# Three of thirteen row one-hot columns made by GpSimd in the routing stage of a graph layer kernel

## The reference, cut to what matters

```python
hi, hj = h[ei], h[ej]                      # ei = src, ej = dst, 103125 edges
m = silu(concat(hi, hj, d2) @ mW1 + mb1)
m = silu(layer_norm(m, ln_g, ln_b) @ mW2 + mb2)
agg = segment_sum(m, ei, 3125)             # sum of the messages of each source node
y = h + silu(concat(h, agg) @ uW1 + ub1) @ uW2 + ub2
...                                        # x + y, then top-k nodes, gelu feed-forward, sum
```

## Time and profile before

| | |
|---|---|
| Runs of the kernel before | 2300.64, 7235.58 and 2305.55 us; median 2305.55 |
| The profiled execution, its time | 2300.03 us |
| The profiled execution, its span | 2298.3 us |
| Busy time, share of the span | PE 2029.3 (88%), DVE 1999.2 (87%), ACT 1385.4 (60%), POOL 1035.3 (45%) |
| Mean granted TensorE clock | 0.947 of full speed |
| First and last scatter of the routing | issued at 192.90 and 411.24 us |

### The profile page before, as it was taken

How to read it: one execution, slowest core, us unless ns; L and a number is a source line. 1 busy time by engine, 2 the same in 40 slices (tenths; PEclk the granted TensorE clock), 3 DMA queues, 4 the chain that set the end, 5 groups by cost and what they waited for, 6 DMA issues and landing times. The chain is left out here.

```text
span 2298.3 us, 51635 instructions
## 1 busy us (share of the span) xinstructions
PE 2029.3 (88%) x11892; PEld 1711.3 (74%) x11893; DVE 1999.2 (87%) x6778; ACT 1385.4 (60%) x2909; POOL 1035.3 (45%) x1037
## 2 busy tenths in 40 slices
PE   3555764499999999999999999999999998799996
PEld 2324553388888888888888888888888886677775
DVE  6899999599999999999999999999999999736795
ACT  1112331388888888787777777777777776423331
POOL 8752222555555555555555555555555556203000
PEclk9987776599999999999999999999999999899998
DMA  3000000432222222222222222222222222010001
GB/s 122 0 1 24 25 25 17 147 94 71 73 71 73 69 73 72 70 73 71 71 73 69 72 71 71 73 71 71 73 71 71 71 70 59 1 40 1 28 1 56
DMA packets 65908, 135.17 MB, mean 59 GB/s; under 512 B 20973, under 2 KB 36451, under 8 KB 65606
## 3 DMA queue, kind: packets, MB, share of 16 engines
q0 software_dynamic: 42016, 111.40, 17.0%
q1 hardware_dynamic: 22577, 22.31, 3.1%
q10 hardware_dynamic: 1266, 0.83, 0.2%
HBM read 124.33 MB, written 10.16 MB: 59 GB/s over the span
## 5 line engine op out<-in xcount | busy, mean ns | idle before, releaser
L862 POOL DMA_INDIRECT g_rows<-b_table,idx_pair x834 | 790.4, 948 | 733.0 <-DVE idx_pair L1014 591.6
L984 PE MATMUL ps<-w2g,nT 128*128 128x256 f32 x3336 | 789.1, 379 | 0.0
L984 PEld LDWEIGHTS ps<-w2g,nT 128*128 128x128 f32 x3336 | 601.5, 190 | 64.5
L899 ACT ACTIVATE normed<-act,shift,rstd_e 128x255 f32<-128x255 f32 x834 | 453.8, 596 | 196.7 <-DVE shift L1086 196.2
L1023 DVE TENSOR_TENSOR agg<-psG,agg 125x256 f32 x834 | 348.4, 418 | 121.6 <-PE psG L967 41.5
L967 PE MATMUL psG<-msg,ohf 128*125 128x256 f32 x1668 | 430.1, 380 | 0.0
L1129 DVE BATCH_NORM_STATS2 stat_e<-act 128x6 f32<-128x256 f32 x834 | 313.8, 423 | 0.0
L958 PE MATMUL psH<-a_sb,ohT 128*128 x1668 | 304.4, 305 | 0.0
L920 ACT ACTIVATE nT<-psM 128x512 f32<-128x512 f32 x417 | 249.0, 597 | 90.1 <-PE psM L976 88.9
L967 PEld LDWEIGHTS psG<-msg,ohf 128*125 128x125 f32 x1668 | 283.9, 187 | 25.1 <-ACT msg L916 0.2
L1122 DVE TENSOR_TENSOR g_rows<-psH,g_rows 128x512 f32<-128x512 f32 x417 | 289.4, 694 | 11.5 <-DMA g_rows<-b_table,idx_pair 8.5
(11 more groups left out here) (201 smaller groups left out, 2406.1 us busy)
## 6 DMA issues: line engine op xcount, KB each, us to landing
g_rows<-b_table,idx_pair POOLq DMA_INDIRECT x834
h_sb<-in_x SPq DMA_DIRECT2D x1, 3125.0 KB
b_table<-b_out SPq DMA_DIRECT2D x25, 125.0 KB
x_all<-in_x SPq DMA_DIRECT2D x1, 3125.0 KB
out<-x_all SPq DMA_DIRECT2D x5, 625.0 KB
rec_d<-rec SPq DMA_DIRECT2D x1, 1668.0 KB, 8.7
agg<-rec_d SPq DMA_DIRECT2D x6, 256.0 KB, 4.2
row<-score_d SPq DMA_DIRECT2D x1, 1525.9 KB
```

The lines of the kernel that those rows point to most:

```text
L862: pool.indirect_dma_start(g_rows[:, j, n, :], None, b_table[:, :], bass.IndirectOffsetOnAxis(ap=idx_pair[:, j, n:n + 1], axis=0)).then_inc ...
L899: ins = nc.scalar.activation(normed[:, (j - 9) % 2, n, 0:D - 1], act1[:, (j - 9) % RING, n, 0:D - 1], ACT.Identity, scale=rstd_e[:, 1 - fa ...
L984: mm = pe.matmul(ps2[:, k, n, :], nT[:, k, n, q, :], w2g[:, q, :], start=(q == 0), stop=(q == 1))
```

## The change: what it does

Of the thirteen row one-hot columns of a group VectorE now makes the first ten, still in one instruction. The last three are made by GpSimd with one `tensor_scalar` per column, which compares the constant row of 0 to 127 (`iota_n`) with the edge's row number, one number per partition. They go to a ring of four, `orp`, that lies in the memory of `f1` and `f2`, which are free by then. `route(s)` waits for both makers. GpSimd makes the columns of groups 0 to 3 as soon as `r_all` and `q_all` are complete (`s_places`), ahead of its `jump` steps, and the columns of group s+4 right behind the issue of scatter s; from group 4 on it first waits for the matmuls of the group that used the ring's place.

```diff
+PCOLS = 3
+PRING = 4
...
-            or_ = sb("or_", [P, 2, COLS, P], BF16)
+            or_ = sb("or_", [P, 2, COLS - PCOLS, P], BF16)
+            orp = [half[:, k * PCOLS * P // 2:(k + 1) * PCOLS * P // 2].bitcast(BF16).rearrange("p (t r) -> p t r", t=PCOLS)
+                   for half in (f1, f2) for k in range(PRING // 2)]
...
+                def pool_columns(s):
+                    if s >= PRING:
+                        pool.wait_ge(s_win, s - PRING + 1)
+                    for k in range(PCOLS):
+                        c = s * COLS + COLS - PCOLS + k
+                        ins = pool.tensor_scalar(orp[s % PRING][:, k, :], iota_n[:, :], r_all[:, c:c + 1], None,
+                                                 ALU.is_equal)
+                    ins.then_inc(s_orp, 1)
+
+                pool.wait_ge(s_places, 1)
+                for s in range(PRING):
+                    pool_columns(s)
                 pool.wait_ge(s_upto, 1)
...
                     pool.indirect_dma_start(rec_d[:, :], bass.IndirectOffsetOnAxis(ap=dest[:, s:s + 1], axis=0),
                                             recw[:, s % 4, :, :].rearrange("p w n -> p (w n)"), None).then_inc(s_scat, 16)
+                    if s + PRING < SUPERS:
+                        pool_columns(s + PRING)
...
                 def route(s):
                     pe.wait_ge(s_or, s + 1)
+                    pe.wait_ge(s_orp, s + 1)
...
-                        mm = pe.matmul(psK[:, s % 3, 0:PLANES * WIN], or_[:, s % 2, t, :],
+                        marks = or_[:, s % 2, t, :] if t < COLS - PCOLS else orp[s % PRING][:, t - COLS + PCOLS, :]
+                        mm = pe.matmul(psK[:, s % 3, 0:PLANES * WIN], marks,
...
-                link(V.tensor_tensor(q_all[:, :], place[:, :], f2[:, :], ALU.subtract))
+                V.tensor_tensor(q_all[:, :], place[:, :], f2[:, :], ALU.subtract).then_inc(s_places, 1)
+                dve.wait_ge(s_places, 1)
...
-                    V.tensor_tensor(or_[:, s % 2, :, :], r_all[:, own].unsqueeze(2).broadcast_to([P, COLS, P]),
-                                    iota_v.unsqueeze(1).broadcast_to([P, COLS, P]), ALU.is_equal)
+                    mine = slice(s * COLS, (s + 1) * COLS - PCOLS)
+                    V.tensor_tensor(or_[:, s % 2, :, :],
+                                    r_all[:, mine].unsqueeze(2).broadcast_to([P, COLS - PCOLS, P]),
+                                    iota_v.unsqueeze(1).broadcast_to([P, COLS - PCOLS, P]), ALU.is_equal)
```

More of the change, by code:

```diff
@@ L223, in build @@
             s_or = sem("s_or")
+            s_orp = sem("s_orp")
+            s_places = sem("s_places")
             s_win = sem("s_win")
```

## The result

The changed kernel takes 2291.68 us (median of 5 runs, 2288.62 to 2293.51), the kernel before 2303.69 in the same series (median of 5 runs, one of which took 7235.58): a ratio of 0.995, 95% interval 0.9934 to 0.9965. So it is faster beyond the noise, but by far less than two per cent, and the forecast of "same" (0.96) came. The forecast time was 2292, range 2281 to 2303. The profiled execution took 2292.16 us, its span is 2290.4.

The account below looks back on a forecast made before the run. VectorE and TensorE's chain of tables at its lower clock were taken to set alternate pairs. Pairs -9.9, columns at the end +1.4, groups 50 to 52 -1.2, start +1.8 gave -7.9 us: 2292, range 2281 to 2303.

Parts of the forecast that it names:

- VectorE's comparison: Row one-hots at L714: 384 of 1664 elements go, 0.397 us less a group, at most 24.6 us over 62 groups.
- The pairs: Middle of the routing, 21 pairs: 11 set by VectorE gain 0.79 us each, 10 by TensorE 1.2 together; 9.9 gained.
- the bound that I gave (12.8): Middle of the routing: 12.8 us gained over the 21 pairs if all TensorE-set pairs last 7.40 us.
- Rival 1: The 21 pairs: TensorE's clock stays up, all last 6.70 us, 20.2 us gained instead of 9.9, time 2282; chance 13%.
- The start: Up to `low(3)`: GpSimd's columns and a lock make it 1.8 us later; bounds 0.2 earlier to 5 later.
- The lock on w2g: Start, L749: two VectorE operations beside GpSimd's 2.8 to 3.0 us steps lose 0 to 5.6 us; 2 taken.
- The columns at the end: Last scatters: five issues with columns behind them, 2.75 us apart against 2.47, lose 1.4 us.
- The end: Groups 50 to 52 gain 1.2 us; VectorE's gain in 53 to 61 is lost to ScalarE's 12.21 us and nine scatters.
- 4: Routing groups: VectorE stands behind GpSimd's columns, kernel over 2% slower, 83 us, time 2383; chance 3%.
- 3: Routing: GpSimd sets the pace from 0.8 us a column on; at 1.0 us the time is 2320; chance 6%.
- 2: The 21 pairs: the clock stays down, every pair lasts 8.22 us, 11.7 us slower, time 2314; chance 4%.
- 5: Whole routing: nothing is left, slow pairs lengthen and the start costs its full 5 us, 2299 to 2303; chance 12%.

Follow-up runs that it names:

- e: The kernel before, with 30 extra matmuls filling TensorE's idle stretch in even groups and all from 50 on: ratio 0.9989 to the kernel before.
- f: The changed kernel with 30 extra matmuls filling TensorE's idle stretch: ratio 0.9942 to the kernel before, 13.6 us less.
- c: The changed kernel without GpSimd's columns, a constant zero matrix in their place (edges of three columns left out): ratio 0.9916 to the kernel before.
- d: The changed kernel with VectorE making all thirteen columns again and GpSimd its three as well: ratio 1.0037 to the kernel before, 7.7 us more.
- a: The changed kernel with VectorE's two w2g operations moved from behind group 2 to behind group 5: ratio 0.9937 to the kernel before.
- h: The changed kernel with the w2g operations behind group 5 and a ring of eight: ratio 0.9925 to the kernel before, 18.6 us less.
- i: The changed kernel again, unaltered, on another chip beside the kernel before: ratio 0.9958, 10.5 us less.
- k: The changed kernel with ScalarE's three small DMAs issued by SyncE instead: ratio 0.9946 to the kernel before, 11.5 us less.
- b: The changed kernel with a ring of eight, columns of groups 4 to 7 made ahead of the first scatter: ratio 0.9929 to the kernel before.
- g: The changed kernel with two columns on GpSimd and eleven on VectorE: ratio 0.9958 to the kernel before, 9.6 us less.
- l: The changed kernel with w2g later, ring of eight, 30 extra matmuls in even groups below 50, small DMAs on SyncE: ratio 0.9918 to the kernel before.

## Why the prediction was right, step by step

*VectorE's comparison*: right, 0.398 us a group against 0.397.

*The pairs*: right in mechanism, mis-sized: 17.3 us against 9.9, and the bound that I gave (12.8) was passed. VectorE's pairs went to 6.70 as said, and eleven of them at 0.79 make the 8.7 us of the sum. The ten that TensorE sets were to give the 1.2 us that they had in hand, and gave 8.6: the mistake was to hold the slow pairs' length fixed. The sign that I gave for it, 1.4 us of waiting in front of `low`, did not come; it is 0.19. A slow pair is as long as the clock stays low in it, and that is no constant of the work: e and f show that the clock costs 3.1 us before and 2.6 after over all 21 pairs, so that VectorE's own 16.8 us (157.82 - 141.02) came through whole, with 0.5 more. c shows that the columns have no part in it, d that the old pattern returns with VectorE's old length. The traces of a, h, i and k have orders of slow pairs different from each other and from after, b and c the order of after, and their sums are all 143.5 to 143.9 us, though i is the same program; with eleven columns on VectorE (g) the clock costs more, 150.86 against some 146.7 of VectorE's own (21 x 6.955 + 0.65). Why the sums agree so well at ten columns is open. Rival 1, the clock stays up, did not come true as a whole: where every second idle stretch is 2.43 us, the clock is low behind it. But for eight pairs of a, and some of k, it did, with stretches of 2.15 us and a clock of 1.00; a pair of 8.13 us then ended it. The gain is nearer to this rival's 20.2 than to 9.9.

*The start*: right in place, too small: 4.9 us against 1.8, just within the bound of 5. The lock on w2g took 4.0 us, within my bounds of 0 and 5.6, of which I took 2; a gives 3.9 back. Its length alone is no price: in i the two operations took 3.44 us and ended at 180.91, as after (180.93), since they end with GpSimd's step. The twelve columns took 10.10 us where I had 7, because the first stood behind VectorE's scan, a lock in the direction that I had not thought of; L473 at 168 to 170 does not follow from 158.5 and 7 us, so that its coming true (168.55) is no merit of the working. The columns behind the first scatters were in the sum and are shown by b (1.2).

*The columns at the end*: 2.8 us against 1.4 for the eight steps from scatter 53 on (22.60 us against 19.79). The column was priced right (three in 1.78 us against 1.74), from rows far from it. The step was not: the issue grew from 0.96 to 1.05, and hand-overs of 0.2 were left out, so 3.05 instead of 2.75.

*The end*: wrong in its cause. I had ScalarE's wait set it; k shows that with ScalarE free the last scatter comes no earlier: one scatter lands late beside the small DMA. What I concluded from it, that VectorE's gain of the last groups is lost, stands.

*The rivals*: 4 is excluded by d for the three operations of a group. The lock on which it rests holds where I put it, at L738 before and at w2g after, and I had seen only half of it: VectorE's operations on SBUF alone stand behind a long step of GpSimd (2.8 to 3.5 us), and a column of GpSimd stands behind a long one of VectorE (3.74 and 2.99 us). A column is so short that an operation behind it loses little (0.16 us in a). 3 did not decide with three columns, and did with four. 2 and 5 did not happen.

*The sum*: the errors were -7.4 (pairs), +3.1 (start), +0.8 (end), together -3.5 at the last scatter. In the profiled pair the difference between executions took just this back. So the parts were off by up to 7.4 us, and that the total met the forecast to a fraction of a us is luck. A small slip besides: 172 to 402 us are slices 4 to 7 of the page, not 3 to 7.

## What to carry to other kernels

Where two engines take turns in setting the length of a step, ask what sets the length of the slow turn: if it is a clock that falls after idle stretches of that engine, as here, it changes with the rhythm, and bounds taken from the old rhythm may be passed. Work moved to an idle engine is not free at the ends of a loop, where it stands in front of what others wait for; make it ahead in time that the engine has (here GpSimd's 13.6 us before the first scatter) and give it a deep enough ring. When moved work shifts GpSimd's or VectorE's long operations on SBUF, look at what the other engine does on SBUF at that time: whichever comes second may stand until the first is over. Here the harm came from the old `jump` steps, shifted beside w2g, and not from the short new columns.

## What the runs showed of the hardware that I had not expected

- Operations of 0.3 us on VectorE with all operands in SBUF (w2g) took 2.3 us each beside GpSimd's `jump` steps of 2.8 us, and 0.38 each beside its columns of 0.6 (a), while operations with an operand in PSUM kept 1457 and 1877 ns.
- The other way round, a GpSimd column of 0.60 us took 3.74 beside VectorE's scan of 3.39 us (after) and 2.99 beside an operation of 3.02 (b).
- With TensorE's idle stretches of 2.15 us in every pair the granted clock was 1.00 (a, 228 to 268 us); with 2.43 in every second pair it was 0.87 in the mean (after).
- The issue of an indirect DMA on GpSimd shows 1.05 us when arithmetic follows it and 0.96 when not.
- A DMA of 3.5 KB in 4-byte pieces landed after 10.2 (l) to 12.1 us (i), and the scatter issued 0.3 us behind it (k) took 10.9 instead of 2.3.
- The same program runs 15 us (0.7%) longer on one chip than on another (2302.47 and 2317.61), so only runs of one chip may be compared at this size.
